# Decay between tokens of a gated delta rule: exp(-|G_t - g_j|) from stored cumulative sums in place of a TensorE product of masked gates

## The chip, the core and the metric

The kernel runs on one core of a Trainium2 chip. The metric is the device time in microseconds of one execution; of three runs before the change the median is 3756.54 us (3755.67 to 3763.35). One execution was profiled; it took 3761.12 us, and its trace spans 3759.3 us.

Engines in the profile: PE is TensorE (PEld its weight loads), DVE VectorE, ACT ScalarE, POOL GpSimd, SP SyncE, which here issues every DMA of the loop. Each runs its own instructions in order and waits on semaphores.

## The reference

The input x has 8 sequences of 1024 tokens, 128 wide. A gated delta-rule attention layer and a feed-forward layer stand one behind the other; each is `x = x + layernorm(layer(layernorm(x)))`. All is float32. The part that matters here, with H = 16 heads, DK = 64, DV = 128:

```python
q, k, v = causal_conv_silu(x @ Wq.T), ..., ...      # 4 taps; q and k are normed over DK
alpha = exp(-exp(A_log) * softplus(x @ Wa.T + dt_bias))
beta = 2.0 * sigmoid(x @ Wb.T)
def step(S, inp):                                   # over the 1024 tokens
    kS = einsum('bhd,bhdv->bhv', k_t, S)
    kkS = einsum('bhd,bhv->bhdv', k_t, kS)
    S = a_t * (S - b_t * kkS) + einsum('bhd,bhv->bhdv', k_t, v_t)
    o_t = einsum('bhdv,bhd->bhv', S, q_t)
o = rms_norm(o) @ Wo.T
```

## The kernel before

The recurrence is computed in chunks of C = 64 tokens. A prologue norms x, transposes it, computes the gates (log alpha in `la`, beta in `be`) and tables of their sums (`tabP`, `tabR`). The main part has STEPS = 128 steps: 8 pairs of heads by 16 chunks, all 8 sequences at once. A tile of 128 partitions holds the 64 tokens of one head in its upper and those of the other in its lower half; along the columns stand the 8 sequences. An epilogue does the feed-forward layer.

A step n runs through three stages, and one pass of the loop does one stage of three neighbouring steps: `l` is finished (inverse applied, output, state S), `m` is in the middle (Gram products, Newton steps for the inverse of a triangular matrix), `n` is begun (projections, convolutions, Gram of k). `pe_body`, `act_body`, `dve_body`, `pool_body` and `sp_body` list what each engine does in a pass, in an order written out by hand; nothing reorders it. 124 passes run in a loop, three bodies stand ahead of it and three behind.

The part that is changed makes the decay between token j and token t of a chunk, the exponential of the sum of log gates between them. Before: POOL multiplies the log gates of step n by two masks (`pool_lm`, tile Lm, 2 x 512 columns); PE multiplies that by triangles of ones, eight products of 256 columns (`pe_dec`, line 513); ACT takes the exponential out of PSUM (`act_exp`, line 726, into ex); POOL multiplies one half by beta over the norm of k (`pool_dmn`, line 995) and the other by the causal mask (`pool_dmp`, line 999). DVE multiplies the Gram product by the first (`dve_n`, line 890, to Nd) and the product of q and k by the second (`dve_p`, line 897, to PT). At the first token of a sequence the gate is set to -1e4 (RESET).

Names on the way: line 502 are the projections (j = 0 to 3: k, q and two halves of v), line 719 the first tap of a convolution on ACT, line 852 the other three on DVE; PE starts projection j + 1 after DVE has done the taps of j, since all use one region of PSUM. Line 696 sums the squares of the output (one-column products), DVE's line 881 reads that, and PE waits for it before line 523, the squared norms of k (one column too). Line 544 is the Gram product of k, line 585 the product N Z, line 611 the product with X0 or X (`pe_z`), line 941 the copy of its diagonal blocks to Z by DVE, line 595 a transpose, line 533 the norms of q, line 706 the output projection, lines 637, 687, 650, 653 are U, the change of S, and the two parts of the output.

Blocks for the inverse go through HBM: `sp_gram` writes Nd (line 1089, scrN), `sp_gram_in` reads 16 x 16 blocks of it (NS), POOL eliminates in them (lines 1047 to 1053), DVE finishes (lines 921 to 931), and SP writes the result (`sp_z_out`, scrZ; `sp_x_out`, line 1108, scrX) and reads it back in another layout: `sp_z_in` (line 1116, Z) and `sp_x_in` (lines 1123 and 1124, X0; the profile calls this tile X). `sp_g` (line 1082) loads two rows of exp(cumulative sum) into every partition of a half of ex, from scrG, which was written once before the loop. A pair of DMAs like this (one for each half) is meant by "pair" below. POOL also scales S (line 1007, Sg) and DVE adds to it (line 960).

Of the kernel before, what the change touches and what calls it, by code (L numbers as in the profile page):

```python
# [15 lines left out]
ALU = mybir.AluOpType  # L16
# [23 lines left out]
RESET = -1.0e4  # L40
# [40 lines left out]
def build(nc, x, wtab, wo, wab, hcol, cst, wf, mu, out):  # L81
    with ExitStack() as ctx:
# [40 lines left out]
        scrX = nc.dram_tensor("scrX", (NB * SB,), F32, kind="Internal").ap()  # L123
        scrG = nc.dram_tensor("scrG", (STEPS, 2, NB * C), F32, kind="Internal").ap()
# [46 lines left out]
        cexp = sig("cexp")  # L171

# [9 lines left out]
        with nc.Block() as block:  # L182
# [32 lines left out]
            def _(dve):  # L215
# [45 lines left out]
                la4 = la[:].rearrange("p (h c b) -> p h c b", h=HP, c=NC)  # L261
                nc.vector.memset(la4[0:1, :, 0, :], RESET)
                then(nc.vector.memset(la4[64:65, :, 0, :], RESET))
# [7 lines left out]
                nc.vector.tensor_copy(tp[:, :, 0:8], v8(la))  # L271
                nc.vector.tensor_scalar(tp[:, :, 8:16], v8(be), -1.0, None, ALU.mult)
                dve.wait_ge(cexp.sem, 1)
                nc.vector.scalar_tensor_tensor(tr[:, :, 0:4], v8(tmp[0])[:, :, 0:4], -1.0, v8(be)[:, :, 0:4], ALU.mult, ALU.mult)
                dve.wait_ge(cexp.sem, 2)
# [77 lines left out]
        g_tr = sig("g_tr")  # L353
        g_cp = sig("g_cp", 2)
        g_out = sig("g_out", 32)
        g_in = sig("g_in", 32)
        lm_ok = sig("lm_ok")
        dec_mm = sig("dec_mm")
# [79 lines left out]
        exN, exP = half(ex, 0), half(ex, 1)  # L438
        CLASSES = (range(0, 4), range(4, 8))
# [643 lines left out]

        def sp_gram(sp, n):
# [67 lines left out]
        def pe_body(pe, l, m, n):  # L1152
# [49 lines left out]
            if m is not None:  # L1202
                if n is not None:
                    pe.wait_ge(dec_ex.sem, dec_ex.at(n))
                else:
                    pe.wait_ge(kt_ok.sem, kt_ok.at(m))
# [32 lines left out]
        def act_body(act, l, m, n):  # L1239
# [112 lines left out]
        with nc.Block() as block:  # L1352
# [277 lines left out]
```

## Time and profile before

| | before |
|---|---|
| median of 3 runs, us | 3756.54 |
| profiled execution, us | 3761.12 |
| its span in the trace, us | 3759.3 |
| mean granted TensorE clock | 0.916 |
| PE busy | 3311.8 us, 88% |
| DVE busy | 2620.1 us, 70% |
| ACT busy | 2675.7 us, 71% |
| POOL busy | 2247.2 us, 60% |
| DMA | 226.12 MB, 60 GB/s |

The busy shares are averages over all stages. An engine at 88% has idle time of a few tenths of a microsecond between groups of instructions; whether such a gap is a wait is told by the row's "[idle before <-releaser]". The granted clock is the share of 2.4 GHz that TensorE was given: 1.00 or 0.50 (1.2 GHz) at a time. Times in the timeline are microseconds from the start of the span; a row merges neighbouring instructions of one kind, with their count.

### The profile page before, as it was taken

How to read it: one execution, taken by the hardware profiler on the slowest of the kernel's cores; microseconds unless marked ns; L12 is line 12 of the kernel's file. 1: busy time of each engine (PE TensorE's matmuls, PEld its weight loads, DVE VectorE, ACT ScalarE, POOL GpSimd, SP SyncE). 2: the span in 40 equal slices, each digit the busy share in tenths (PEclk: the TensorE clock that was granted, in tenths of full speed). 3: DMA queues.
4: the chain of work that ended last, by engine and by line, in shares of the span. 5: the costliest groups of instructions: out<-in, count | busy, mean ns of one | idle time of the engine just before them, and what ended most of it. 6: DMA issues, size and time to landing. Idle time of an engine off the chain costs nothing. (4 is left out here: it accounts for less than half of the span.)

```text
span 3759.3 us, 195058 instructions
## 1 busy us (share of the span) xinstructions
PE 3311.8 (88%) x77978; PEld 2756.6 (73%) x77978; DVE 2620.1 (70%) x5529; ACT 2675.7 (71%) x5548; POOL 2247.2 (60%) x3494
## 2 busy tenths in 40 slices
PE   5699999999999999999999999999999999999665
PEld 4577777777777777777777777777777777777433
DVE  5677777777777777777777777777777777777254
ACT  2577777777777777777777777777777777777433
POOL 1366666666666666666666666666666666666211
PEclk9799999999999999999999999999999999999767
DMA  2232323233232323233232323233232323323111
GB/s 60 51 67 57 69 56 67 59 63 62 61 65 58 69 54 69 61 62 64 59 69 54 70 57 66 59 63 69 54 69 56 67 57 65 62 60 66 34 34 40
DMA packets 911057, 226.12 MB, mean 60 GB/s; under 512 B 820128, under 2 KB 894112, under 8 KB 911008
## 3 DMA queue, kind: packets, MB, share of 16 engines
q1 hardware_dynamic: 910848, 224.91, 28.5%
q8 instruction: 33, 0.54, 0.1%
q0 software_dynamic: 160, 0.53, 0.0%
q14 instruction: 16, 0.13, 0.0%
HBM read 169.73 MB, written 55.58 MB: 60 GB/s over the span
## 5 line engine op out<-in xcount | busy, mean ns | idle before, releaser
L852 DVE SCALAR_TENSOR_TENSOR cv<-ps,w_kq,cv 128x512 f32<-128x512 f32 x768 | 575.6, 750 | 419.2 <-ACT cv L719 405.6
L852 DVE SCALAR_TENSOR_TENSOR cv<-ps,w_v,cv 128x512 f32<-128x512 f32 x768 | 575.7, 750 | 152.8 <-ACT cv L719 134.7
L1016 POOL TENSOR_TENSOR accT<-accT,X 128x512 f32 (+1 forms) x128 | 163.5, 1277 | 533.3 <-ACT Y L817 533.3
L502 PE MATMUL ps<-xnT,w_kq 128*128 (+1 forms) x1024 | 327.6, 445 | 74.6 <-DVE cv L852 68.9
L502 PE MATMUL ps<-xnT,w_v 128*128 (+1 forms) x1024 | 330.8, 448 | 14.2 <-DVE cv L852 14.1
L976 POOL TENSOR_TENSOR sc<-tabP,sc 128x8 f32<-128x8 f32 x128 | 26.1, 204 | 510.5 <-DVE sc L867 510.5
L1007 POOL TENSOR_TENSOR Sg<-S,tabR 128x512 f32<-128x512 f32 x256 | 329.9, 1307 | 0.0
L765 ACT ACTIVATE Vt<-ps,sc 128x128 f32<-128x128 f32 x1024 | 277.8, 382 | 54.9 <-PE ps L571 54.9
L706 PE MATMUL ps<-wo_s,oo 128*128 128x128 f32 x2048 | 312.9, 314 | 0.6 <-issue 0.6
L967 POOL TENSOR_TENSOR Lm<-k_all,tabP 128x512 f32<-128x512 f32 x256 | 280.3, 1114 | 30.5 <-POOLq L182 30.5
L706 PEld LDWEIGHTS ps<-wo_s,oo 128*128 128x128 f32 x2048 | 288.1, 225 | 14.1 <-issue 0.9
L952 DVE SCALAR_TENSOR_TENSOR Rr<-ps,sc,Vt 128x128 f32<-128x128 f32 x1024 | 288.3, 345 | 1.4
L637 PEld LDWEIGHTS ps<-Rr,Z 64*64 64x64 f32 x4096 | 243.7, 144 | 56.2 <-issue 56.2
L696 PEld LDWEIGHTS ps<-k_all,KB 128*128 128x128 f32 x2048 | 239.9, 193 | 58.9 <-issue 58.9
L502 PEld LDWEIGHTS ps<-xnT,w_kq 128*128 128x128 f32 x1024 | 184.1, 199 | 126.6 <-issue 93.2
L637 PE MATMUL ps<-Rr,Z 64*64 64x128 f32 x4096 | 274.8, 288 | 1.9 <-issue 1.9
L696 PE MATMUL ps<-k_all,KB 128*128 128x1 f32 x2048 | 247.4, 251 | 5.9 <-ACT KB L802 2.1
L585 PEld LDWEIGHTS ps<-Z,NM 64*64 64x64 f32 x8192 | 189.2, 168 | 81.1 <-issue 81.0
L585 PE MATMUL ps<-Z,NM 64*64 64x64 f32 x8192 | 215.4, 256 | 31.4 <-DVE Z L941 29.1
L808 ACT ACTIVATE oo<-ps 128x1024 f32<-128x1024 f32 x128 | 131.1, 1024 | 156.6 <-PE ps L653 156.6
L653 PE MATMUL ps<-PT,U 64*64 64x64 f32 x8192 | 217.4, 221 | 23.4 <-PE ps L650 22.8
L817 ACT ACTIVATE X<-ps,sc 128x128 f32<-128x128 f32 x512 | 145.9, 368 | 121.1 <-PE ps L706 120.7
(198 smaller groups left out, 8537.2 us busy)
## 6 DMA issues: line engine op xcount, KB each, us to landing
ex<-scrG SPq DMA_DIRECT2D x256, 128.0 KB, 2.9
scrN<-Nd SPq DMA_DIRECT2D x256, 128.0 KB, 2.6
Z<-scrZ SPq DMA_DIRECT2D x256, 128.0 KB, 3.2
X<-scrX SPq DMA_DIRECT2D x512, 64.0 KB
w_kq<-wtab SPq DMA_DIRECT2D x128, 132.0 KB, 2.2
w_v<-wtab SPq DMA_DIRECT2D x128, 132.0 KB, 2.5
wo_s<-wo SPq DMA_DIRECT2D x128, 128.0 KB, 2.8
NS<-scrN SPq DMA_DIRECT2D x128, 64.0 KB, 2.6
```

Source lines behind the costliest of these rows:

```text
L502: last = nc.tensor.matmul(pj[:, 4 * g:4 * g + 4, 0:CW], w[:, (j % 2) * P:(j % 2 + 1) * P], xnT3[:, 4 * g:4 * g + 4, bass.ds((n % NC) * C, ...
L585: last = nc.tensor.matmul(ps[place(cls, a), col64(PB["y1" if l else "y0"], cls, i)], blk64(BD["NM"], b, a), blk64(BD["Z"], b, a), start=Tr ...
L637: last = nc.tensor.matmul(ps[a:z, col128(PB["u"], g, i)], blk64(BD["Z"], b, a), unit(Rr, b)[a:z], start=True, stop=True)
L653: last = nc.tensor.matmul(o_cols(h ^ cls, b, d), U[a:z, b * P + d:b * P + d + 64], blk64(BD["PT"], b, a), start=False, stop=(b == NB - 1))
L696: last = nc.tensor.matmul(ps[:, (PB["ms"] + h) * 512 + i:(PB["ms"] + h) * 512 + i + 1], osq[:, h * 512 + i * P:h * 512 + (i + 1) * P], kc( ...
L706: last = nc.tensor.matmul(ps[:, col128(PB["wo"], h, i)], oo[:, h * 512 + i * P:h * 512 + (i + 1) * P], wo_s[:, h * D:(h + 1) * D], start=T ...
L765: last = nc.scalar.activation(unit(Vt, b), unit(ps, 4 * PB["vtr"] + b), ACT.Copy, scale=rv[:, b:b + 1])
L852: nc.vector.scalar_tensor_tensor(cv4[:, j], pj[:, :, k:k + C], tap(j, k), cv4[:, j], ALU.mult, ALU.add).then_inc(conv[j].sem, 1)
L952: last = nc.vector.scalar_tensor_tensor(unit(Rr, b), ps[:, col128(PB["ks"], g, i)], cr[:, b:b + 1], unit(Vt, b), ALU.mult, ALU.add)
L967: last = nc.gpsimd.tensor_tensor(v3(Lm, i), over(kc(o, C), NB, C), tabP3[:, bass.ds(n, 1), 0:8].rearrange("p o b -> p b o").to_broadcast([ ...
L1007: nc.gpsimd.tensor_tensor(half(Sg, g).rearrange("p (b v) -> p b v", b=4), half(S, g).rearrange("p (b v) -> p b v", b=4), gam, ALU.mult).th ...
L1016: nc.gpsimd.tensor_tensor(dst, dst, row(yt[h]), ALU.add).then_inc(acc_ok.sem, 1)
```

## The change

The cumulative sums G of the log gates within a chunk are already computed in the prologue, in PSUM (banks 0 to 3). After the change they are kept: for each token in a column of `tabP` (g_j, in place of the log gate), and, transposed, as one row for each step and half in a new HBM tensor scrD. In each step SP loads the two rows of scrD into all 64 partitions of their half of Lm (`sp_d`), POOL subtracts the column (`pool_d`), ACT takes the absolute value and then the exponential with scale -1 (`act_abs`, `act_exp`), in place in SBUF. The gates fall along the tokens, so -|G_t - g_j| is the wanted sum on either side of the diagonal. `pe_dec` and the masks of POOL are gone. The first chunk's reset is done by zeroing table entries in the prologue. Waits of `act_exp` for the readers of ex move to `pool_dmn` and `pool_dmp`.

```diff
@@ the tables, on DVE in the prologue
-                nc.vector.memset(la4[0:1, :, 0, :], RESET)
-                then(nc.vector.memset(la4[64:65, :, 0, :], RESET))
...
-                nc.vector.tensor_copy(tp[:, :, 0:8], v8(la))
...
+                dve.wait_ge(cexp.sem, 2)
+                nc.vector.tensor_copy(tp[:, :, 0:4], bank(0, 2).rearrange("p (n k) -> p n k", k=8)[:, :, 0:4])
+                nc.vector.tensor_copy(tp[:, :, 4:8], p4(6)).then_inc(d_tab.sem, 1)
...
+                then(nc.vector.memset(first_chunk(tmp[0][:], 8), 0.0))
+                dve.sem_inc(g_tab.sem, 1)
+                then(nc.vector.memset(first_chunk(tabR[:], 16)[:, :, 4:16], 0.0))
@@ TensorE
-        def pe_dec(pe, n):
-            pe.wait_ge(lm_ok.sem, lm_ok.at(n))
-            pe.sem_inc(pe_go.sem, 1)
-            for i, o in enumerate((K_LE, K_GT)):
-                for cls in range(2):
-                    for a, z in HALF:
-                        c = (PB["dec"] + cls) * 512 + i * 4 * C
-                        last = nc.tensor.matmul(ps[place(cls, a), c:c + 4 * C], k_all[a:z, o + a:o + z],
-                                                Lm[a:z, i * 512 + cls * 4 * C:i * 512 + (cls + 1) * 4 * C], start=True, stop=True)
-            last.then_inc(dec_mm.sem, 1)
@@ ScalarE
+        def act_abs(act, n):
+            act.wait_ge(d_ok.sem, d_ok.at(n))
+            nc.scalar.activation(Dt, Dt, ACT.Abs).then_inc(d_abs.sem, 1)
+
         def act_exp(act, n):
-            act.wait_ge(dec_mm.sem, dec_mm.at(n))
-            if not first(n):
-                act.wait_ge(nd_ok.sem, nd_ok.at(n - 1))
-                act.wait_ge(pt_ok.sem, pt_ok.at(n - 1))
-            nc.scalar.activation(ex[:, 0:1024].rearrange("p (i g n) -> p g i n", i=2, g=2),
-                                 bank(PB["dec"], 2).rearrange("p (g i n) -> p g i n", g=2, i=2), ACT.Exp).then_inc(dec_ex.sem, 1)
+            act.wait_ge(d_abs.sem, d_abs.at(n))
+            nc.scalar.activation(Dt, Dt, ACT.Exp, scale=-1.0).then_inc(dec_ex.sem, 1)
@@ GpSimd
-        def pool_lm(pool, n):
-            if not first(n):
-                pool.wait_ge(dec_mm.sem, dec_mm.at(n - 1))
+        def pool_d(pool, n):
+            pool.wait_ge(d_in.sem, d_in.at(n))
+            if not first(n):
+                pool.wait_ge(dmn_ok.sem, dmn_ok.at(n - 1))
+                pool.wait_ge(dmp_ok.sem, dmp_ok.at(n - 1))
             pool.sem_inc(pool_go.sem, 1)
-            for i, o in enumerate((K_MGT, K_MLE)):
-                last = nc.gpsimd.tensor_tensor(v3(Lm, i), over(kc(o, C), NB, C),
...
+            nc.gpsimd.tensor_tensor(v3(Lm, 1), v3(Lm, 0),
+                                    tabP3[:, bass.ds(n, 1), 0:8].rearrange("p o b -> p b o").to_broadcast([P, NB, C]),
+                                    ALU.subtract).then_inc(d_ok.sem, 1)
@@ SyncE
+        def sp_d(sp, n):
+            if not first(n):
+                sp.wait_ge(d_ok.sem, d_ok.at(n - 1))
+            sp.sem_inc(sp_go.sem, 1)
+            for h, (a, z) in enumerate(HALF):
+                sp.dma_start(half(Lm, 0)[a:z], scrD[bass.ds(n, 1), h, :].to_broadcast([C, NB * C])).then_inc(d_in.sem, 16)
@@ before the loop: SP, ACT and PE (eight more transposes, two copies, two writes)
+            for h, n in enumerate(("Z", "X0")):
+                sp.wait_ge(d_cp.sem, d_cp.at(0, h + 1))
+                sp.dma_start(scrD[:, h, :], half(BD[n], 1)).then_inc(d_out.sem, 16)
...
+            sp.wait_ge(d_out.sem, d_out.at(0))
@@ the bodies
         def sp_body(sp, l, m, n):
+            if n is not None:
+                sp_d(sp, n)
             if l is not None:
                 sp_x_in(sp, l)
...
-                pe_dec(pe, n)
```

Three places in the order of the instructions show it. First PE in the loop, around the product that goes; S and sl are the state and the convolved k, KB the squared output, sq squares. Before:

```order
L626 MATMUL ps<-S,sl 64x128 [waits s1_ok,silu_k,s0_ok]
L626 MATMUL ps<-S,sl 64x128 x15
L507 REGISTER_ALU [waits kt_ok]
L513 MATMUL ps<-Lm,k_all 64x256 [waits lm_ok]
L513 MATMUL ps<-Lm,k_all 64x256 x7
L696 MATMUL ps<-k_all,KB 128x1 [waits pt_ok,osq_ok]
L696 MATMUL ps<-k_all,KB 128x1 x7
L523 MATMUL ps<-k_all,sq 64x1 [waits ro_in,sq_k]
L523 MATMUL ps<-k_all,sq 64x1 x15
L502 MATMUL ps<-xnT,w_v 128x4x67 [waits conv_q,wv_in]
```

and now, from the same product with S on:

```order
L623 MATMUL ps<-S,sl 64x128 [waits s1_ok,silu_k,s0_ok]
L623 MATMUL ps<-S,sl 64x128 x15
L693 MATMUL ps<-k_all,KB 128x1 [waits pt_ok,osq_ok]
L693 MATMUL ps<-k_all,KB 128x1 x7
L515 REGISTER_ALU [waits ro_in]
L520 MATMUL ps<-k_all,sq 64x1 [waits sq_k]
L520 MATMUL ps<-k_all,sq 64x1 x15
```

Line 513 is gone with its wait for POOL, and line 696 (now 693) follows the product with S at once; line 523 (now 520) still waits for ro_in, which DVE signals.

Second SP at the head of a pass, where X stands for X0, w_kq for the weights of k and q, and Nd for the Gram product. Before:

```order
L1346 UNCONDITIONAL_BRANCH
L1346 ISA
L1121 ISA [waits x_out]
L1123 DMA X<-scrX 64x4x64 [waits z_mm]
L1124 DMA X<-scrX 64x4x64
L1123 DMA X<-scrX 64x4x64
L1124 DMA X<-scrX 64x4x64
L1061 ISA
L1063 ISA [waits conv_q]
L1063 DMA w_kq<-wtab 128x264
L1089 DMA scrN<-Nd 64x8x64 [waits n_in,nd_ok]
```

and now:

```order
L1353 UNCONDITIONAL_BRANCH
L1353 ISA
L1091 ISA [waits d_ok]
L1091 DMA Lm<-scrD 64x512
L1091 ISA
L1091 DMA Lm<-scrD 64x512
L1128 ISA
L1130 ISA [waits x_out]
L1132 DMA X<-scrX 64x4x64 [waits z_mm]
L1133 DMA X<-scrX 64x4x64
L1132 DMA X<-scrX 64x4x64
L1133 DMA X<-scrX 64x4x64
```

The pair from scrD stands ahead of the four DMAs of X0 and of all that comes behind them.

Third ACT, where sl is the convolved k, sq its square, and sc holds the small columns of norms. Before:

```order
L719 ACTIVATE cv<-ps,w_kq 128x512 [waits silu_q,proj_q]
L730 ISA
L736 ACTIVATE sl<-cv 128x512 [waits k_tr,gram_p,ks_mm,gram_k,conv_k]
L742 ACTIVATE sq<-sl 128x512 [waits nk_mm,silu_k]
L1260 ACT_TABLE_LOAD
L726 ACTIVATE ex<-ps 128x2x2x256 [waits pt_ok,nd_ok,dec_mm]
L825 ACTIVATE sc<-sc 128x8 [waits v_ok,n2_ok]
```

and now:

```order
L733 ACTIVATE sl<-cv 128x512 [waits k_tr,gram_p,ks_mm,gram_k,conv_k]
L739 ACTIVATE sq<-sl 128x512 [waits nk_mm,silu_k]
L720 ACTIVATE Lm<-Lm 128x512 [waits d_ok]
L1267 ACT_TABLE_LOAD
L724 ACTIVATE Lm<-Lm 128x512 [waits d_abs]
L822 ACTIVATE sc<-sc 128x8 [waits v_ok,n2_ok]
L826 ACTIVATE sc<-sc 128x8 [waits rv_ln]
```

The exponential out of PSUM has become an Abs ahead of the table load and an exponential behind it, each of 512 columns.

## Rows read from the trace of the kernel before

**Rows 1.** Timeline of PE: last group of line 653 in five steps (start, us).

```profile
613.89 0.69 PE L653 MATMUL ps<-PT,U 64*64 64x64 f32 x32 [0.18 <-PE ps L650]
...
639.08 0.69 PE L653 MATMUL ps<-PT,U 64*64 64x64 f32 x32 [0.18 <-PE ps L650]
...
665.45 0.69 PE L653 MATMUL ps<-PT,U 64*64 64x64 f32 x32 [0.18 <-PE ps L650]
...
693.43 0.69 PE L653 MATMUL ps<-PT,U 64*64 64x64 f32 x32 [0.18 <-PE ps L650]
...
719.73 0.69 PE L653 MATMUL ps<-PT,U 64*64 64x64 f32 x32 [0.18 <-PE ps L650]
```

**Rows 2.** Windows: stretch, length, busy by engine, then granted clock, DMA share, GB/s.

```profile
614.60:639.80 25.20, 22.80 (x601) 19.28 (x601) 18.93 (x38) 20.06 (x42) 16.20 (x27) 1.00 0.33 65
...
614.60:720.50 105.90, 97.24 (x2401) 81.91 (x2402) 76.56 (x149) 80.09 (x169) 68.63 (x109) 0.94 0.31 62
647.70:651.10 3.40, 3.40 (x69) 2.49 (x68) 2.19 (x8) 2.63 (x6) 2.66 (x4) 0.50 0.50 111
...
685.30:688.70 3.40, 3.40 (x20) 2.50 (x21) 0.73 (x1) 1.97 (x4) 2.93 (x9) 0.50 0.00 0
```

**Rows 3.** Groups of instructions by line, shapes apart: busy us, mean ns.

```profile
L513 PE MATMUL ps<-Lm,k_all 64*64 64x256 f32 x2048 | 139.1, 381 | 2.4 <-DVE KT L903 1.6 <-POOL Lm L967 0.5
...
L726 ACT ACTIVATE ex<-ps 128x1024 f32<-128x1024 f32 x128 | 131.0, 1023 | 1.4
...
L742 ACT ACTIVATE sq<-sl 128x512 f32<-128x512 f32 x128 | 80.7, 630 | 4.0
```

**Rows 4.** Timeline of DVE: last two taps of q, then line 881.

```profile
644.15 1.53 DVE L852 SCALAR_TENSOR_TENSOR cv<-ps,w_kq,cv 128x512 f32<-128x512 f32 x2
...
646.40 0.17 DVE L881 TENSOR_TENSOR sc<-ps,sc 128x8 f32<-128x8 f32 x1 [0.71 <-PE ps L696]
```

**Rows 5.** Timeline of SP's queue, 618 to 626 us.

```profile
618.01 1.28 SPq L1116 DMA_DIRECT2D Z<-scrZ  x2
619.55 1.21 SPq L1082 DMA_DIRECT2D ex<-scrG  x2
...
623.32 0.62 SPq L1124 DMA_DIRECT2D X<-scrX  x1
624.38 0.34 SPq L1063 DMA_DIRECT2D w_kq<-wtab  x1
625.26 1.28 SPq L1089 DMA_DIRECT2D scrN<-Nd  x2
```

**Rows 6.** DMA issues: count, KB each, median us from issue to landing.

```profile
ex<-scrG SPq DMA_DIRECT2D x256, 128.0 KB, 2.9
...
Z<-scrZ SPq DMA_DIRECT2D x256, 128.0 KB, 3.2
...
w_kq<-wtab SPq DMA_DIRECT2D x128, 132.0 KB, 2.2
...
scrX<-XB SPq DMA_DIRECT2D x128, 64.0 KB, 2.6
```

**Rows 7.** Timeline of PE: the product with X0, step of 25.19 us.

```profile
626.60 0.69 PE L611 MATMUL ps<-Y,X 64*64 64x64 f32 x32 [0.27 <-ACT Y L780]
```

**Rows 8.** The same product in the step of 27.98 us.

```profile
679.34 0.69 PE L611 MATMUL ps<-Y,X 64*64 64x64 f32 x32
```

**Rows 9.** Timeline of DVE: the update of S and what follows it.

```profile
640.04 1.29 DVE L960 TENSOR_TENSOR S<-ps,Sg 128x512 f32<-128x512 f32 x2 [0.18 <-POOL Sg L1007]
...
641.70 0.69 DVE L903 TENSOR_TENSOR KT<-ps,tabP 128x512 f32<-128x512 f32 x1 [0.37 <-PE ps L564]
...
642.89 0.75 DVE L852 SCALAR_TENSOR_TENSOR cv<-ps,w_kq,cv 128x512 f32<-128x512 f32 x1 [0.50 <-ACT cv L719]
```

**Rows 10.** Timeline of SP's queue before the loop.

```profile
93.31 0.36 SPq L1129 DMA_DIRECT2D scrG<-Y  x1
95.63 0.34 SPq L1063 DMA_DIRECT2D w_kq<-wtab  x1
```

More of the change, by code:

```diff
@@ L123, in build @@
         scrX = nc.dram_tensor("scrX", (NB * SB,), F32, kind="Internal").ap()
+        scrD = nc.dram_tensor("scrD", (STEPS, 2, NB * C), F32, kind="Internal").ap()
         scrG = nc.dram_tensor("scrG", (STEPS, 2, NB * C), F32, kind="Internal").ap()
@@ L171, in build @@
         cexp = sig("cexp")
+        d_tab = sig("d_tab")
+        g_tab = sig("g_tab")
         xt = [KBuf for KBuf in (BD["KB"], BD["QG"])]
@@ L352, in build @@
         wo_in = sig("wo_in", 16)
-        g_tr = sig("g_tr")
+        g_tr = sig("g_tr", 2)
         g_cp = sig("g_cp", 2)
+        d_cp = sig("d_cp", 2)
         g_out = sig("g_out", 32)
         g_in = sig("g_in", 32)
-        lm_ok = sig("lm_ok")
-        dec_mm = sig("dec_mm")
+        d_out = sig("d_out", 32)
+        d_in = sig("d_in", 32)
+        d_ok = sig("d_ok")
+        d_abs = sig("d_abs")
         dec_ex = sig("dec_ex")
@@ L438, in build @@
         exN, exP = half(ex, 0), half(ex, 1)
+        Dt = half(Lm, 1)
         CLASSES = (range(0, 4), range(4, 8))
@@ L994, in pool_dmn @@
             pool.wait_ge(bn_ok.sem, bn_ok.at(n))
-            nc.gpsimd.tensor_tensor(v3(ex, 0), v3(ex, 0), bcast(bn, C), ALU.mult).then_inc(dmn_ok.sem, 1)
+            if not first(n):
+                pool.wait_ge(nd_ok.sem, nd_ok.at(n - 1))
+            nc.gpsimd.tensor_tensor(v3(ex, 0), v3(Lm, 1), bcast(bn, C), ALU.mult).then_inc(dmn_ok.sem, 1)
         def pool_dmp(pool, n):
             pool.wait_ge(dec_ex.sem, dec_ex.at(n))
-            nc.gpsimd.tensor_tensor(v3(ex, 1), v3(ex, 1), over(kc(K_MLE, C), NB, C), ALU.mult).then_inc(dmp_ok.sem, 1)
+            if not first(n):
+                pool.wait_ge(pt_ok.sem, pt_ok.at(n - 1))
+            nc.gpsimd.tensor_tensor(v3(ex, 1), v3(Lm, 1), over(kc(K_MLE, C), NB, C), ALU.mult).then_inc(dmp_ok.sem, 1)
         def pool_sg(pool, m):
@@ L1082, in sp_g @@
                 sp.dma_start(half(ex, 2)[a:z], scrG[bass.ds(n, 1), h, :].to_broadcast([C, NB * C])).then_inc(g_in.sem, 16)
+        def sp_d(sp, n):
+            if not first(n):
+                sp.wait_ge(d_ok.sem, d_ok.at(n - 1))
+            sp.sem_inc(sp_go.sem, 1)
+            for h, (a, z) in enumerate(HALF):
+                sp.dma_start(half(Lm, 0)[a:z], scrD[bass.ds(n, 1), h, :].to_broadcast([C, NB * C])).then_inc(d_in.sem, 16)
         def sp_gram(sp, n):
@@ L1202, in pe_body @@
             if m is not None:
[L1203 to L1206, printed above, removed]
+                pe.wait_ge(kt_ok.sem, kt_ok.at(m))
                 pe_y(pe, m, 0)
@@ L1321, in pool_body @@
             if n is not None:
-                pool_lm(pool, n)
+                pool_d(pool, n)
             if m is not None:
@@ L1365, in _ @@
                 act.preload_act_table_set("silu_and_others")
+                act.wait_ge(g_tr.sem, g_tr.at(0, 1))
+                for h, n in enumerate(("Z", "X0")):
+                    nc.scalar.activation(v3(BD[n], 1), bank(2, 2).rearrange("p (b h t) -> p b h t", b=NB, h=2)[:, :, h, :],
+                                         ACT.Copy).then_inc(d_cp.sem, 1)
                 act.wait_ge(g_tr.sem, g_tr.at(0))
@@ L1378, in _ @@
                 for b in range(NB):
+                    last = nc.tensor.transpose(unit(ps, 8 + b), tabP3[:, :, b], ident)
+                last.then_inc(g_tr.sem, 1)
+                for b in range(NB):
                     last = nc.tensor.transpose(unit(ps, 16 + b), tmp[0][:].rearrange("p (n b) -> p n b", b=NB)[:, :, b], ident)
                 last.then_inc(g_tr.sem, 1)
+                pe.wait_ge(d_cp.sem, d_cp.at(0))
                 pe.wait_ge(g_cp.sem, g_cp.at(0))
```

14 lines of the change are left out of this document (3 added, 11 removed).

## The prediction

> **What bounds the kernel now.** I read the engine table first, then the timeline of four neighbouring steps, then its windows for the clock, and last the two engines that meet there, TensorE (PE) and the queue of SyncE (SP). A "step" is one pass of the loop; I count it from the start of the last 32 products of line 653, which end every step. Five such starts lie 25.19, 26.37, 27.98 and 26.30 us apart [rows 1]: a beat of 105.84 us, 26.46 us a step. The windows say why the four differ [rows 2]: over the beat the granted clock is 0.94, and inside it stand stretches at 0.50 (1.2 GHz instead of 2.4). The shortest step has none. A first kind of stretch (647.7 to 651.1, and one like it in each of the next two steps) comes right behind the one-column products of lines 696 and 523; a second kind (685.3) stands in the 27.98 step alone, behind line 533, also one-column products. A stretch of the first kind costs 26.30 - 25.19 = 1.11 us, the second kind 27.98 - 26.30 = 1.68 us. PE is busy in nearly all of the rest, so this is a PE-bound loop whose queue is fed in a fixed order: what counts is which wait on PE ends last, place by place. There are 124 passes of the loop, and three bodies before and three behind them.
>
> **What goes: the product of masked gates.** Per step PE loses the eight products of line 513: 139.1 us over 128 steps, 1.09 us each [rows 3]. If PE alone bound, that is -136 us. It does not follow, since behind it PE waits for VectorE (DVE). Line 696 would start 1.1 us earlier and end 1.1 us earlier, but line 523 waits for DVE's line 881, and DVE does the three taps of the q convolution first: they end at 644.15 + 1.53 = 645.68, while line 881 starts now at 646.40, after an idle 0.71 us [rows 4]. So at most 0.7 of the 1.09 us passes this place; the rest is a new wait of PE for DVE.
>
> **What ScalarE (ACT) gets.** One exponential of 1024 columns from PSUM (1023 ns) becomes an Abs and an Exp of 512 each in SBUF; the nearest row is line 742, 630 ns [rows 3]. 2 x 0.63 - 1.02 = +0.24 us. The Abs stands ahead of the table load, so the Exp ends some 0.25 us later than now. Both ends: 0 (there is idle time before line 825) and 0.25 us. I take 0.25: it leaves 0.7 - 0.25, about 0.4 us, of the gain for what comes after. GpSimd (POOL) replaces two products by one subtraction, at a place where it isn't waited for; it gains about 1 us that nobody needs.
>
> **What SP gets.** Two DMAs of scrD into Lm per step, of the same form as the pair from scrG into ex (64 rows of 2 KB each out of one row): 1.21 us of issue, and 0.26 us between the end of the pair before (618.01 + 1.28) and its start [rows 5]. 1.47 us a step. Their data are wanted some 20 us later, so the transfer is hidden. The queue behind them is not: they stand at the head of the body, ahead of the four DMAs that bring X0 from scrX, then w_kq, then the pair that writes Nd out. SP runs without a pause from the issue of scrX to the last of the four (they follow one another at 618.01, 619.55, ... 623.32), so the four move by the full 1.47 us: the last one starts at 624.79 instead of 623.32. How long it takes to land the page doesn't say of this one; its twin in size, scrX<-XB of 64 KB, takes 2.6 us, and the ends are w_kq, 2.2, and Z, 3.2 [rows 6]. With 2.6: X0 is there at 625.9 now and at 627.39 after.
>
> Line 611 (the product of X0 with Y) starts at 626.60 in the step without a slow stretch [rows 7]. Now X0 has 0.7 us to spare; after, PE stands there until 627.4, 0.8 us later than now, whatever it gained before. With the landing at 2.2 it is 0.4 us, at 3.2 it is 1.4 us. Does the delay stay on the path? DVE's copy of Z follows the product, and line 585 needs the copy, then come line 595, 533 and 611 again, the v projection's taps, and the next step. Each waits for the one before; there is no slack after line 611 in this step. So 25.19 + 0.8 = 26.0 us.
>
> In the steps with a slow stretch of the first kind line 611 comes later anyway: at 679.34, 13.9 us after its step's start at 665.45, against 12.7 in the free step [rows 1, 7, 8]. X0 after the change: 627.4 - 613.89 = 13.5. There the 0.4 us gained before does count: 26.3 becomes 25.9, and as the slow stretch can now begin earlier and lie over more of the v projection (line 502), I give 0.1 back: 26.0. So X0 makes all steps equal at 26.0 us, but for the second kind of slow stretch.
>
> The third thing on SP: the pair that writes Nd starts at 625.26 now, right when Nd is ready; after, SP comes to it at 624.38 + 0.34 + 1.47 + 0.1, about 626.3, +1.0 us. It feeds POOL's elimination, after which POOL scales S, and DVE's update of S at 640.04 already waits 0.18 us for that [rows 9]. It moves to 641.1 where the step's end moves to 640.6: 0.5 us late. DVE has waits of 0.37 and 0.50 us before the next two operations, so I price it at 0, with 0.3 us as the other end.
>
> **The clock.** Taking 1.09 us of dense products out from right before the one-column products leaves the thin stretch longer: lines 696 and 523 with a wait between. The row shows the clock at 0.50 after this place in three steps of four [rows 2]; it will be all or nearly all, which costs nothing more, since X0 hides it (above). What decides is the second kind, in one step of four now. PE's new wait before line 611 stands ahead of it, and as the steps become equal their phase is a new one. Bounds: never (0) and every step (1.68 us). I take 0.35 instead of 0.25 of the steps.
>
> The Trainium skill (TensorE: Matmul & The Clock Gate, What's actually happening) says that the slow clock is the default and activity releases it. By that rule removing dense products and adding a wait can only bring more slow stretches; rows 2 agree as far as they go, every fall stands behind one-column products.
>
> **The sum.** A step after: 26.0 + 0.35 x 1.68 = 26.6 us, against 26.46: +0.14, times 124 = +17 us. The prologue: eight more transposes ahead of the eight of G, two ACT copies and two more writes to HBM before the wait for both (scrG is issued at 93.31, w_kq at 95.63 after it has landed [rows 10]): about 2 us; the first pair from scrD ahead of w_kq, for which PE waits: 1.5 us; two copies out of PSUM and two memsets in DVE's chain: 2 us, an estimate from 0.6 to 0.7 us for 512 columns [rows 3, 4]; together +5.5. Own time of the profiled execution 3761.1 + 17 + 5.5 = 3784. The median of the runs is 3756.5, 4.6 below that execution. **Forecast: 3780 us.**
>
> **Rivals.**
> 1. *The queue of SP isn't the bound; the kernel is faster.* X0 lands in 2.2 us or less and SP catches up somewhere, so that PE keeps what passes DVE, 0.3 to 0.4 us a step: 0.35 x 124 = 43, minus 5.5: 3756.5 - 38 = 3718 us. For it: 1.09 us of PE work really goes from the bounding engine. Against: SP's rows have no gap in which 1.47 us fit between scrX and X0 [rows 5]. The Trainium skill (DMA: Bandwidth & Descriptors, Issuing engines are not separate DMA queues) calls the sequencer's time to start a DMA usually small beside the DMA; here a pair holds SP 1.21 us, and one of the pair lands in 2.9 [rows 5, 6]. By that rule this rival is the forecast.
> 2. *The clock.* The second kind of slow stretch comes in three steps of four: 26.0 + 0.75 x 1.68 = 27.3, +0.8 x 124 = +100, and with the prologue 3860 us. It decides from one step in two on (26.84, +0.38 x 124 = +47, 3809). For it: the thin part of the step grows; against: it falls in a part of the step that the edit itself leaves as it is.
> 3. *No change.* The loss in the free step and the gain in the others cancel, with the second kind still in one of four: 26.0 + 0.42 = 26.42, -5 us in the loop, +5.5 in the prologue: 3757 us.
>
> **Chances.** Forecast (3765 to 3810) 0.48, rival 1 0.22, rival 2 0.17, rival 3 0.13. What a measurement can tell from no change is about 0.2%, 7.5 us. Faster 0.22, same 0.13, slower 0.65. The range takes rival 1 down to 3715 and rival 2 up to 3850: landing times of 2.2 and 3.2 us alone move the free step by -0.4 and +0.6 us, and one step in ten more or less of the second kind is 21 us.
>
> **What would show it.** Line 611's first product waiting for the DMA X<-scrX in most steps, and starting 13.5 us after the step's start in nearly all of them; the four X0 issues 1.47 us later against scrX's; Nd's write starting about 1 us after Nd is ready; DVE's update of S waiting for POOL; line 523 still waiting for DVE's line 881; the count of slow stretches of the second kind a beat. Wrong if PE doesn't wait for X0 (then rival 1), or if the steps are equal at 26.0 and yet the time is far from 3780 (then the clock).

## The result, and the profile after

| | before | after |
|---|---|---|
| median, us | 3756.78 (3755.67 to 3763.35, 4 runs) | 3881.47 (3875.72 to 3882.07, 4 runs) |
| ratio to before | | 1.0325 [1.0307, 1.0343] |
| span of the profiled execution, us | 3759.3 | 3879.8 |
| mean granted TensorE clock | 0.916 | 0.881 |
| PE busy | 3311.8 us | 3311.0 us |

The kernel became 3.3% slower. I had forecast 3780 us with a range from 3715 to 3850: the sign was right, the size was not. After the change the lines have moved: 653 is now 650, 696 is 693, 523 is 520, 533 is 530, 611 is 608, DVE's 881 and 897 are 878 and 894, SP's 1124, 1063 and 1089 are 1133, 1065 and 1098.

Timeline of PE in the kernel after, four steps (start us, length us, engine, line, operation, out<-in, tile, type, count [idle before <-releaser]):

```profile
1615.56 0.69 PE L650 MATMUL ps<-PT,U 64*64 64x64 f32 x32 [0.18 <-PE ps L647]
...
1643.26 0.69 PE L650 MATMUL ps<-PT,U 64*64 64x64 f32 x32 [0.18 <-PE ps L647]
...
1671.33 0.69 PE L650 MATMUL ps<-PT,U 64*64 64x64 f32 x32 [0.18 <-PE ps L647]
...
1676.64 1.92 PE L693 MATMUL ps<-k_all,KB 128*128 128x1 f32 x16 [0.90 <-DVE PT L894]
1679.01 0.64 PE L520 MATMUL ps<-k_all,sq 64*64 64x1 f32 x32 [0.45 <-DVE sc L878]
...
1697.80 0.69 PE L650 MATMUL ps<-PT,U 64*64 64x64 f32 x32 [0.18 <-PE ps L647]
...
1725.89 0.69 PE L650 MATMUL ps<-PT,U 64*64 64x64 f32 x32 [0.18 <-PE ps L647]
```

The steps are 27.70, 28.07, 26.47 and 28.09 us long. Before they were 25.19, 26.37, 27.98 and 26.30 [rows 1]. The short one is gone, and two of the four are about 28.

Windows of the kernel after (stretch, length, busy of PE, PEld, DVE, ACT, POOL, then granted clock, DMA share, GB/s): the four steps, then the slow stretches in the first, third and fourth of them.

```profile
1616.30:1726.60 110.30, 97.95 (x2337) 83.17 (x2337) 78.69 (x149) 80.62 (x172) 65.78 (x106) 0.89 0.32 69
1622.10:1628.80 6.70, 6.25 (x108) 5.15 (x107) 3.50 (x14) 4.24 (x8) 2.98 (x5) 0.50 0.54 151
1680.20:1683.40 3.20, 3.20 (x68) 2.39 (x67) 2.00 (x7) 2.50 (x7) 2.77 (x4) 0.50 0.51 132
1707.50:1710.70 3.20, 3.20 (x65) 3.08 (x59) 2.48 (x6) 2.94 (x4) 2.57 (x4) 0.50 0.47 107
1717.70:1721.00 3.30, 3.30 (x18) 2.39 (x20) 0.49 (x1) 2.02 (x4) 2.64 (x10) 0.50 0.00 0
```

Beside the two kinds of slow stretch known from before [rows 2] there is a long form of the first: from 1622.1 to 1628.8, twice as long, beginning while line 693 still runs. The lengths of 120 inner steps, each from one start of the last group of line 650 (653 before) to the next:

| steps | before | after |
|---|---|---|
| no slow stretch | 32 of 25.19 us | 1 of 25.75 |
| first kind alone | 61 of 26.33 | 49 of 26.43 |
| first kind, long | none | 32 of 27.70 |
| first and second kind | 27 of 27.99 | 37 of 28.09 |
| long and second | none | 1 of 29.63 |
| mean, us | 26.40 | 27.30 |

From the first such start to the last, 3361.9 us before and 3478.3 after: +116.4 us lie in the steps, some 108 of them in these 120 and some 8 in the first and the last few. Of the rest of the +120.5 by which the span grew, 4.0 us lie ahead of them, and nothing behind.

By this table the +0.90 us a step is made up of four parts. Before, 32 steps were 1.14 us shorter than those with the first kind alone, and all but one of these are gone: 0.30. After, 33 steps have the long form, 1.27 us each: 0.35. Eleven more have the second kind, 1.66 us each: 0.15. And with the same slow stretch a step is 0.10 us longer than before.

Waits of the kernel after (who waited for whom: us in total, times, longest):

```profile
PE ps L693 <- DVE PT L894: 112.7, 125, 0.9
...
PE ps L520 <- DVE sc L878: 56.8, 126, 0.5
```

and its line 608, by line (busy us, mean ns | idle before, by releaser):

```profile
L608 PE MATMUL ps<-Y,X 64*64 64x64 f32 x8192 | 179.2, 225 | 4.6 <-DMA X<-scrX 4.4 <-ACT Y L777 0.2
```

These rows together are the balance. The removed products were 139.1 us of PE [rows 3], and yet PE's busy time is the same (3311.8 and 3311.0 us): the remaining work took that much longer at the lower mean clock (0.881 for 0.916). Where the products stood, line 693 now waits for DVE's P^T, for 112.7 us in all, a wait that the kernel before does not have. PE's idle time, span less busy, grew from 447.5 to 568.8 us, by 121.3 us, which is the whole loss. PE waits for X0 for 4.4 us in the whole run; it isn't X0 that made the kernel slow.

A small part of the loss has nothing to do with the clock. Before, line 523 starts 0.15 us after DVE's line 881 has ended; now line 520 starts 0.25 us after the end of line 878, in every one of the 120 steps, and PE's wait for it grew from 44.1 to 56.8 us:

```profile
PE ps L523 <- DVE sc L881: 44.1, 126, 0.4
```

That is the 0.10 us between 26.33 and 26.43. In the order of the instructions the wait for ro_in has moved from the product itself to an instruction of its own ahead of it (L515 REGISTER_ALU); that this is what takes the 0.1 us was not tested.

### The profile page after: what moved, and what is told of

Read it like the earlier page. It is cut to its first block and busy times, and to the rows that moved or that the text cites. A ratio compares the mean times of both kernels' runs of the same rounds, so it can differ in the third digit from the quotient of the medians.

```text
span 3879.8 us, 191739 instructions
## 1 busy us (share of the span) xinstructions
PE 3311.0 (85%) x75938; PEld 2780.3 (72%) x75938; DVE 2663.5 (69%) x5530; ACT 2692.0 (69%) x5678; POOL 2124.0 (55%) x3366
## 5 line engine op out<-in xcount | busy, mean ns | idle before, releaser
L510 PE MATMUL ps<-xnT,w_kq 128*128 (+1 forms) x1024 | 337.5, 456 | 76.8 <-DVE cv L849 68.9
L693 PE MATMUL ps<-k_all,KB 128*128 128x1 f32 x2048 | 264.7, 259 | 114.9 <-DVE PT L894 112.7
L510 PE MATMUL ps<-xnT,w_v 128*128 (+1 forms) x1024 | 356.1, 476 | 4.2 <-DVE cv L849 4.1
L693 PEld LDWEIGHTS ps<-k_all,KB 128*128 128x128 f32 x2048 | 257.5, 204 | 142.2 <-issue 142.2
L703 PE MATMUL ps<-wo_s,oo 128*128 128x128 f32 x2048 | 328.0, 324 | 1.4 <-DVE Rr L949 1.4
L703 PEld LDWEIGHTS ps<-wo_s,oo 128*128 128x128 f32 x2048 | 303.5, 235 | 16.3 <-issue 1.6
L1009 POOL TENSOR_TENSOR Sg<-S,tabR 128x512 f32<-128x512 f32 x256 | 308.6, 1226 | 0.0
L582 PEld LDWEIGHTS ps<-Z,NM 64*64 64x64 f32 x8192 | 202.2, 178 | 88.9 <-issue 88.9
L582 PE MATMUL ps<-Z,NM 64*64 64x64 f32 x8192 | 227.6, 267 | 38.3 <-DVE Z L938 38.3
L1018 POOL TENSOR_TENSOR accT<-accT,Y 128x512 f32 (+1 forms) x128 | 242.0, 1891 | 0.2 <-issue 0.2
```

What stands on the lines that cost most here:

```text
L510: last = nc.tensor.matmul(pj[:, 4 * g:4 * g + 4, 0:CW], w[:, (j % 2) * P:(j % 2 + 1) * P], xnT3[:, 4 * g:4 * g + 4, bass.ds((n % NC) * C, ...
L582: last = nc.tensor.matmul(ps[place(cls, a), col64(PB["y1" if l else "y0"], cls, i)], blk64(BD["NM"], b, a), blk64(BD["Z"], b, a), start=Tr ...
L693: last = nc.tensor.matmul(ps[:, (PB["ms"] + h) * 512 + i:(PB["ms"] + h) * 512 + i + 1], osq[:, h * 512 + i * P:h * 512 + (i + 1) * P], kc( ...
L703: last = nc.tensor.matmul(ps[:, col128(PB["wo"], h, i)], oo[:, h * 512 + i * P:h * 512 + (i + 1) * P], wo_s[:, h * D:(h + 1) * D], start=T ...
L1009: nc.gpsimd.tensor_tensor(half(Sg, g).rearrange("p (b v) -> p b v", b=4), half(S, g).rearrange("p (b v) -> p b v", b=4), gam, ALU.mult).th ...
L1018: nc.gpsimd.tensor_tensor(dst, dst, row(yt[h]), ALU.add).then_inc(acc_ok.sem, 1)
```

## The experiments

The theory after the result: the loss is TensorE's clock, which falls behind the products of one column (lines 693, 520 and 530), and removing the dense products in front of them only laid bare more of it. Its rival is my forecast's own mechanism, the longer queue of SP. "Widened" means that a product of one column gets 64 or 128 equal columns. Each experiment's ratio is to the kernel before, run on the same chip in the same job.

| kernel | median, us | ratio [95%] | mean step, us | none | first | long | second |
|---|---|---|---|---|---|---|---|
| before | 3756.78 | 1 | 26.40 | 32 | 88 | 0 | 27 |
| after | 3881.47 | 1.0325 [1.0307, 1.0343] | 27.30 | 1 | 86 | 33 | 38 |
| e1_fill | 3832.48 | 1.0196 [1.0143, 1.0249] | 26.98 | 16 | 88 | 4 | 44 |
| e2_spmove | 3875.88 | 1.0307 [1.0284, 1.0329] | 27.30 | 0 | 91 | 29 | 41 |
| e4_before_wide | 3625.46 | 0.9649 [0.9626, 0.9671] | 25.35 | 120 | 0 | 0 | 0 |
| e7_ms4 | 3875.71 | 1.0315 [1.0290, 1.0340] | 27.30 | 0 | 68 | 52 | 67 |
| e5_after_wide | 3700.14 | 0.9853 [0.9837, 0.9870] | 25.93 | 120 | 0 | 0 | 0 |
| e6_wide_sp | 3642.34 | 0.9701 [0.9682, 0.9721] | 25.43 | 120 | 0 | 0 | 0 |
| e8_all | 3535.47 | 0.9418 [0.9402, 0.9435] | 24.57 | 120 | 0 | 0 | 0 |
| e9_wide_first | 3815.36 | 1.0176 [1.0151, 1.0201] | 26.79 | 48 | 0 | 0 | 72 |
| e10_wide_nq | 3877.41 | 1.0323 [1.0288, 1.0357] | 27.31 | 0 | 40 | 80 | 0 |
| e11_wide_ms4 | 3717.56 | 0.9889 [0.9856, 0.9922] | 26.05 | 101 | 0 | 0 | 0 |

The last four columns count, in 120 inner steps of the profiled execution, those without a slow stretch, those with the first kind in its short and in its long form (beginning up to 10.5 us after a step's end of line 650, or its like), and those with the second kind (from 16.5 us on). e11 has 19 steps with a stretch between the two, at 14 us.

**e1_fill: the dense products back, and nothing else.** After, with eight products of 256 columns on constants at the old place, into PSUM banks that nobody reads then.

```diff
+    if m is not None:
+        pe.wait_ge(kt_ok.sem, kt_ok.at(m))
+    pe_fill(pe, n)     # 8 products 64x256, k_all x k_all, banks 4 and 5
     if l is not None:
```

> The changed kernel with eight products of 256 columns put back where the old ones stood, on constants, their result used by nobody; all else (loads, subtraction, Abs and Exp) as changed. Theory clock: the products gave no time as work, but they kept TensorE's clock up ahead of the one-column products; steps without a slow stretch come back, PE then waits for X0 in them: 25.9, 26.4, 28.0, 26.4 us, about 3795 us. Rival SP queue (the loss is the late X0 and Nd): nothing changes or it gets 0.1 us a step worse, 3880 to 3895 us.

Measured 3832 us. Adding work that nobody needs makes the kernel 1.3% faster, which no queue explains, and the mean clock rises from 0.881 to 0.905; so far the theory holds. But the size is short of the 3795. Steps without a slow stretch came back in 16 of 120, not in 32, and they last 25.85 us, not 25.19: X0 is late in them. e1's line 617 (608 of after) waits for it:

```profile
PE ps L617 <- DMA X<-scrX: 34.6, 31, 3.7
```

So dense products ahead of the thin ones help the clock here, and don't secure it. The same products at another place weren't tried, so this run alone doesn't tell whether it is their place that counts.

**e2_spmove: the two loads of scrD behind everything that this step needs.**

```diff
 def sp_body(sp, l, m, n):
-    if n is not None:
-        sp_d(sp, n)
     ...
         sp_gram_in(sp, m)
+    if n is not None:
+        sp_d(sp, n)
```

> The changed kernel with the pair of loads from scrD issued later in SP's body, behind the read of the 16x16 blocks (where SP waits anyway), so that X0, w_kq and Nd are issued as before the change. Theory clock: X0 is hidden behind the slow stretch in nearly every step, so 3870 to 3882 us. Rival SP queue: the whole loss goes, about 3765 us.

The last issue of X0 ends 1.4 us earlier in the step than after the change, the mean step stays at 27.30, the time is 3876 us. The queue, as the kernel stands, costs nothing of note. The rival's 3765 is out.

**e4_before_wide: the kernel before, thin products made wide.** The moving operand has 64 or 128 equal columns, of which one is read.

```diff
-  nc.tensor.matmul(ps[:, (PB["ms"] + h) * 512 + i:(PB["ms"] + h) * 512 + i + 1],
-                   osq[:, ...], kc(K_ONE, 1), start=True, stop=True)
+  nc.tensor.matmul(ps[:, col128(PB["ms"], h, i)],
+                   osq[:, ...], kc(K_ONE), start=True, stop=True)
```

and likewise lines 523 and 533 with 64 columns.

> The kernel before the change, with the sums of squares (lines 523, 533, 696) taken by moving tiles of 64, 64 and 128 equal columns instead of one; the first column of each result is read. The same number of instructions, the same values. Theory clock: nearly all slow stretches go, all steps as the free one, 25.2 us: 3757 - 1.25 x 124 = about 3600 us. Rival (slow stretches come with the time of the step or with waits, not with one-column products): the wider tiles cost 0.1 to 0.3 us a step, 3770 to 3795 us.

Measured 3625 us, 3.5% faster than before; 25 us more than expected, since the step is 25.35 us, not 25.2. Timeline of its PE, and a window over four steps:

```profile
1603.49 0.69 PE L653 MATMUL ps<-PT,U 64*64 64x64 f32 x32 [0.18 <-PE ps L650]
...
1608.80 2.02 PE L696 MATMUL ps<-k_all,KB 128*128 128x128 f32 x16
1611.17 0.69 PE L523 MATMUL ps<-k_all,sq 64*64 64x64 f32 x32 [0.35 <-DVE sc L881]
...
1628.81 0.69 PE L653 MATMUL ps<-PT,U 64*64 64x64 f32 x32 [0.18 <-PE ps L650]
```
```profile
1603.00:1704.00 101.00, 92.09 (x2396) 76.94 (x2388) 75.41 (x149) 80.27 (x169) 68.61 (x109) 1.00 0.32 65
```

Sixteen products of 128 columns take 2.02 us, of one column 1.92 at the full clock; 32 of 64 columns 0.69 instead of 0.64. For a tenth of a microsecond here and there the clock stays at 2.4 GHz through all 120 steps. The waits in this place are the same as in the free step before (0.35 us for line 881), so it is the columns, not the waits. The Trainium skill (TensorE: Matmul & The Clock Gate, HAM oscillation — how this bites in real kernels) describes a clock that swings because the engine stands idle for DMA. That is another case than this one: after the change, PE stands idle for 0.45 us in all, and not for a DMA, between the start of line 693 at 1676.64 and the fall at 1680.2; and e5_after_wide, below, keeps both idle gaps of this place (113.2 and 56.7 us in all, 112.7 and 56.8 after), and has no slow stretch in 120 steps.

**e7_ms4: the wait for P^T taken away.** The sums of line 693 go to PSUM banks 4 and 5, which are free once DVE has copied K^T; in banks 2 and 3 they had to wait for P^T to be read.

```diff
-PB = {..., "ms": 2, "wo": 6}
+PB = {..., "ms": 4, "wo": 6}
-            pe.wait_ge(pt_ok.sem, pt_ok.at(m))
+            pe.wait_ge(kt_ok.sem, kt_ok.at(m))
         pe_ms(pe, l)
```

> The changed kernel with the sums of the squared output (line 693) written to PSUM banks 4 and 5, which the removed products freed, so that they need not wait for DVE's PT but only for KT. Theory clock: PE's wait of 0.9 us ahead of them goes, but the thin stretch gets no denser; line 520 waits for DVE's line 878 instead, some 0.6 us earlier than now: between 3800 (the 0.6 us counts) and 3881 us (the slow stretches take it back); I expect 3830. Rival (the wait for PT is the whole loss): below 3790 us.

A miss: the time lies inside the two bounds, but at the end where nothing is gained, not at 3830. The wait is gone, and line 693 starts 4.34 us after the group's start instead of 5.31, but the time is what it was. Timeline of its PE, then the two slow stretches in the second step:

```profile
2051.16 0.69 PE L650 MATMUL ps<-PT,U 64*64 64x64 f32 x32 [0.18 <-PE ps L647]
2055.50 1.95 PE L693 MATMUL ps<-k_all,KB 128*128 128x1 f32 x16
...
2076.86 0.69 PE L650 MATMUL ps<-PT,U 64*64 64x64 f32 x32 [0.18 <-PE ps L647]
...
2105.73 0.69 PE L650 MATMUL ps<-PT,U 64*64 64x64 f32 x32 [0.18 <-PE ps L647]
```
```profile
2083.80:2090.50 6.70, 6.70 (x108) 5.66 (x109) 4.56 (x14) 5.06 (x10) 2.98 (x5) 0.50 0.56 142
2097.50:2100.80 3.30, 3.30 (x18) 2.39 (x20) 0.49 (x1) 2.07 (x4) 2.79 (x8) 0.50 0.00 0
```

The steps are mostly 25.8, 27.3 and 28.8 us long: those with the short first kind alone are 0.64 us shorter than after the change (25.79 for 26.43), and the clock, at 0.861, takes all of it back, with the second kind in 67 steps for 38. Removing work or waits from PE does not pay here while the clock falls.

**e5_after_wide, e6_wide_sp, e8_all: the change at full clock, one cover after the other.** e5 widens lines 693, 520 and 530 of the changed kernel as e4 does; e6 adds e2's move; e8 adds e7's banks as well.

> The changed kernel, but lines 520, 530 and 693 multiply by 64, 64 and 128 equal columns in place of one (only one of them is read). Theory (the lost time is TensorE's clock, which falls where the products have one column): no stretch with a clock of 1.2 GHz stays in the loop. Then the transfer of the value projection (X0, which lands 12.5 us after the end of a step's value chain) sets every step, at about 25.8 us as in the few full-clock steps of e1_fill, 1.5 us under the 27.3 of the changed kernel: about 3695 us (3680 to 3710). Rival A, the late transfer binds nothing even at full clock: 25.35 us a step as in e4_before_wide, about 3635 us. Rival B, the clock's fall comes from the removed products alone and not from the one-column ones: 3840 to 3880 us.

> As e5_after_wide, and the two decay loads of the next chunk moved on SP's queue behind the transfers that this step needs. If the late X0 is what e5_after_wide's steps wait for, these go to 25.35 us as in e4_before_wide and the whole to its 3625 us and some 8 to 12 us of longer prologue: 3635 to 3640 us. If X0 doesn't bind there, this is the same as e5_after_wide within 5 us.

> As e6_wide_sp, and the sums of the squared output go to PSUM banks that the matrices of the tail don't use, so that TensorE doesn't wait for DVE's copy of P^T (as in e7_ms4). Theory (the removed 1.09 us of products lay in the shadow of that wait, and comes out once both the wait and the clock's falls are gone): a step of 24.7 to 24.9 us, 3560 to 3590 us. Rival (something behind the q convolution, GpSimd's S or the transfers, sets the step at once): 25.35 us as e6_wide_sp, 3635 us.

e5 came to 3700 (expected 3695), e6 to 3642 (3635 to 3640). Line 608 in both, by line, e5 first:

```profile
L608 PE MATMUL ps<-Y,X 64*64 64x64 f32 x8192 | 178.6, 224 | 101.3 <-DMA X<-scrX 100.2 <-issue 0.8 <-ACT Y L777 0.3
```
```profile
L608 PE MATMUL ps<-Y,X 64*64 64x64 f32 x8192 | 178.6, 224 | 37.6 <-ACT Y L777 33.0 <-DMA X<-scrX 3.4 <-issue 1.1
```

With the clock out of the way X0 does bind, for 100.2 us, 0.8 a step; with the pair moved on SP, PE waits for X0 for 3.4 us, and the kernel is 58 us faster. A step of e5, timeline of PE:

```profile
1773.94 0.69 PE L650 MATMUL ps<-PT,U 64*64 64x64 f32 x32 [0.18 <-PE ps L647]
1779.25 2.02 PE L693 MATMUL ps<-k_all,KB 128*128 128x128 f32 x16 [0.90 <-DVE PT L894]
...
1787.28 0.69 PE L608 MATMUL ps<-Y,X 64*64 64x64 f32 x32 [0.64 <-DMA X<-scrX]
...
1799.73 0.69 PE L650 MATMUL ps<-PT,U 64*64 64x64 f32 x32 [0.18 <-PE ps L647]
```

e5 against e4 is the change as it was made, with both kernels at full clock: 3700 against 3625 us, +75 us (2.1% by the ratios) instead of the +125 with the clock falling, and 58 of the 75 go with the pair's place on SP. With the clock falling the same move was worth some 6 us at most (e2; the intervals overlap). So the clock and the late X0 can't be booked side by side.

e6 against e4 is the change alone, at full clock and with its queue put right: 0.9701 [0.9682, 0.9721] against 0.9649 [0.9626, 0.9671], each to the kernel before in its own job; it is slower by 0.5%, mostly the 0.08 us a step. That is about the 0.09 us by which line 520 starts later in e6 than line 523 in e4 (medians of 7.78 and 7.69 us into the step). The removed 1.09 us a step are worth nothing there: the wait for P^T stands in their place (e6: 113 us), and line 693 starts 5.31 us into the step in e6, as line 696 does in e4 (5.32). e8 takes that wait away and comes to 3535 us, under its expected 3560 to 3590, and 5.8% under the kernel before. Its PE:

```profile
1670.10 0.69 PE L650 MATMUL ps<-PT,U 64*64 64x64 f32 x32 [0.18 <-PE ps L647]
...
1674.43 2.05 PE L693 MATMUL ps<-k_all,KB 128*128 128x128 f32 x16
1677.01 0.69 PE L520 MATMUL ps<-k_all,sq 64*64 64x64 f32 x32 [0.53 <-DVE sc L878]
...
1694.64 0.69 PE L650 MATMUL ps<-PT,U 64*64 64x64 f32 x32 [0.18 <-PE ps L647]
```

24.54 us a step: of the 0.98 us by which line 693 starts earlier 0.85 us arrives at the mean step. This is where the gain of the removed products had been: it takes the wide columns, the moved pair and the other banks together. Before, the same banks held their result until the exponential had read it, so e8's step isn't open to the kernel before as it stands; a version of that kernel with other banks wasn't tried.

**e9_wide_first and e10_wide_nq: which thin products.** e9 widens lines 693 and 520 only, e10 line 530 only.

> As e5_after_wide, but only lines 520 and 693 are widened; the norms of q at line 530 keep one column. Theory (each run of one-column products brings its own fall of the clock): the slow stretch at 6 to 9 us into a step is gone, the one at 18 to 20 us stays, in about one step in three; steps of 25.8 and of about 27.5 us: some 3770 us (3740 to 3800). Rival (line 530 doesn't matter, the first run of one-column products alone starts both): as e5_after_wide, about 3695 us.

> The changed kernel with only line 530 (the norms of q) widened to 64 equal columns; lines 520 and 693 keep one. The counterpart of e9_wide_first. If each run of one-column products brings its own fall of the clock, the slow stretch at 18 to 20 us into a step goes and the one at 6 to 9 us stays in every step: about 26.4 us a step, 3775 us (3755 to 3795). If it is the sum of the thin products over a step that counts, wherever they stand, stretches stay at both places, and the time lies between 3790 and 3860 us.

Windows of e9 over a slow stretch and the whole step around the next but one; then of e10 over two slow stretches and the two steps around them:

```profile
746.90:750.20 3.30, 3.30 (x26) 2.61 (x27) 1.63 (x3) 2.12 (x4) 2.64 (x10) 0.50 0.00 0
...
782.60:809.90 27.30, 23.63 (x585) 19.83 (x585) 19.70 (x37) 20.44 (x43) 16.08 (x26) 0.94 0.34 70
```
```profile
1563.50:1570.20 6.70, 6.25 (x106) 5.14 (x107) 3.90 (x13) 4.43 (x9) 2.98 (x5) 0.50 0.54 144
1594.20:1597.50 3.30, 3.30 (x62) 3.18 (x54) 2.58 (x5) 2.88 (x4) 2.51 (x4) 0.50 0.51 117
1557.40:1611.50 54.10, 48.01 (x1168) 40.97 (x1168) 38.24 (x75) 40.22 (x86) 31.93 (x53) 0.91 0.33 71
```

"Run" here means a row of one-column products behind one another. As to places both say the same: each such row brings its own stretch. In e9 the first kind is gone from all steps, in e10 the second. As to the time both missed. e9 has the second kind in 72 of 120 steps, not in one of three (3815 us for 3770). e10 lost the second kind altogether and gained nothing (3877 for 3775): 80 of its 120 steps have the long form of the first kind, against 33 after. The two don't add up. Taking one away moves the steps against the clock, and the other comes more often or lasts longer; only without both is the time gone. What sets how often they come, and why some are twice as long, these runs don't show.

**e11_wide_ms4: the wait gone, X0 still late.** e5 with e7's banks.

> As e5_after_wide, and the sums of the squared output in banks 4 and 5 as in e8_all, but the decay loads of the next chunk stay ahead of X0 on SP's queue. If X0's landing 12.5 us into the step sets e5_after_wide's steps, then taking away TensorE's wait for P^T buys nothing: 25.8 us a step, 3700 us as e5_after_wide. If that wait is worth the 0.85 us a step by which e8_all is under e6_wide_sp, whatever X0 does: about 3595 us.

3718 us: nothing gained over e5. It is 0.4% slower, measured in another job; a slow stretch is back in 19 steps. By line:

```profile
L608 PE MATMUL ps<-Y,X 64*64 64x64 f32 x8192 | 180.5, 226 | 208.4 <-DMA X<-scrX 207.1 <-issue 0.8 <-ACT Y L777 0.5
```

207.1 us of waiting for X0 are about e5's 100.2 and the 113 us that it had at P^T, moved to one place.

## Why the prediction was wrong

**What failed first: "What goes".** I let 0.7 of the removed 1.09 us pass, up to DVE's line 881. But line 696 itself waits for P^T; that wait stood with it in the order of the program, and I priced only what came behind it. In the free step before, line 696 starts 619.21 - 613.89 = 5.32 us after the group; after, 1676.64 - 1671.33 = 5.31. Timeline of the kernel before, PE and DVE, then of DVE after:

```profile
618.09 1.07 PE L513 MATMUL ps<-Lm,k_all 64*64 64x256 f32 x16
...
618.38 0.68 DVE L897 TENSOR_TENSOR PT<-ps,ex 128x512 f32<-128x512 f32 x1
...
619.21 1.92 PE L696 MATMUL ps<-k_all,KB 128*128 128x1 f32 x16
```

```profile
1675.81 0.68 DVE L894 TENSOR_TENSOR PT<-ps,ex 128x512 f32<-128x512 f32 x1
```

DVE ends P^T at 619.06 before and at 1676.49 after, 5.17 and 5.16 us into the step, and in both kernels the one-column products start 0.15 us later; over the 120 steps the medians are the same, 5.16 and 5.31. Nothing of the 1.09 us passed. The removed products, which end at 619.16, had lain beside DVE's work on P^T to the last, and the row of before showed no wait only because they filled it. So "0.4 us left", and with it "26.3 becomes 25.9" in the slow steps, falls: they are 26.43.

**What failed second: "The clock".** I wrote that the first kind in nearly all steps "costs nothing more, since X0 hides it". It is in all but one, and it costs: X0 would have held a step at 26.0 by the forecast (25.9 in e5), and the slow stretch makes it 26.43. And I had no long form of it, 27.70 - 26.43 = 1.27 us more, in 33 of 120 steps. The frequency of the second kind, 0.35 a step, was about right: 38 of 120, 0.32, at 28.09 - 26.43 = 1.66 us, for my 1.68. That was luck: no row gave the 0.35, and the equal steps by which I argued for it did not come. With the measured terms the step is 26.43 + 0.32 x 1.66 + 0.275 x 1.27 = 27.31, against 27.30 measured and 26.6 forecast; the missing 0.7 us is 0.43 from the first kind (which holds the failed step above) and 0.35 from its long form, less 0.06 from the second. Rival 2 named the clock and 27.3 us a step, but by the second kind in three steps of four; that is not what happened.

**The sign.** "Slower" came true, but not for the reason given. The forecast's +17 us in the loop rested on X0 holding every step at 26.0 us, and on the 0.35 for which no row spoke; PE waits for X0 only twice, for 4.4 us in all. That the sign was right is largely luck.

**What was right but hidden: SP and X0.** The pair takes 1.14 us of issue (timeline of SP, L1091), the last X0 issue moves by 1.25 us for my 1.47, and line 608 starts 1787.28 - 1773.94 = 13.34 us into e5's step for my 13.5. The step that this gives, 26.0, is 25.93 in e5's mean. The mechanism is shown, its price is 58 us (e5 against e6), and in the changed kernel it is covered by the slow clock. The Trainium skill (DMA: Bandwidth & Descriptors, Issuing engines are not separate DMA queues) calls the sequencer's time to start a DMA usually small beside the DMA itself. Here the pair takes 1.14 us to issue and one of it lands 2.8 us after its issue (median of Lm<-scrD), and its place on SP is worth 1.6% once nothing covers it.

**The rest.** ACT's Abs delays the exponential by 0.1 us, not 0.25. The write of Nd is late by 0.8 us (1.0 forecast), and it does cost nothing: DVE's line 957 waits for POOL 1.3 us in the whole run (line 960 before: 6.0). The prologue: w_kq is issued at 99.71 instead of 95.63 [rows 10], +4.1 for my 5.5:

```profile
98.40 1.21 SPq L1091 DMA_DIRECT2D Lm<-scrD  x2
99.71 0.52 SPq L1065 DMA_DIRECT2D w_kq<-wtab  x1
```

Of the two signs that I named for being wrong, "the steps are equal at 26.0 and yet the time is far" and "PE doesn't wait for X0", the second came true, but with a slower kernel instead of a faster one behind it: I had not thought that something slower than X0 could cover it.

## What to carry to other kernels

A row of an engine without a wait may be filled exactly by the work that you remove: look at the semaphores of the instruction behind it, and at when their releaser ends, before a microsecond is booked as gain. On a PE-bound loop read the granted clock first: where it falls behind one-column products, try to widen these (three lines, -3.5% here) before any work is taken from PE; in this loop what was taken out until then came back as a slower clock (the change itself, and e7). A late transfer, a wait and a slow clock cover one another; their prices show only with the others removed, and gains come in jumps when the last cover goes (under e5: e11 nothing, e8 165 us).

## What the runs showed of the hardware

- The width of the moving tile decided over the clock in this loop, at nearly no cost in time. Mean of one product of line 696, 128x1 in the kernel before and 128x128 in e4: 251 ns at a mean clock of 0.916, 282 ns at 0.972; for its 16, 1.92 against 2.02 us at full clock. The columns don't set the pace of these products. The weight loads beside them take 193 ns each in both kernels, and in the step at 613.89 they are busy for 1.86 of the 1.92 us; that they set it was not tested.
- Work whose result nobody reads made a kernel faster (e1, 3832 against 3881 us), with the mean clock at 0.905 for 0.881.
- In two kernels the clock's falls repeat with the loop: before, they mostly come again every four steps [rows 1, 2], in e10 every three, without an exception in 120 (two steps of 27.72 and one of 26.48). After the change no such beat holds: steps of 28.09 and 26.43 us alternate for a while, then some of 27.70 come in between; in e1, e7 and e9 the order is irregular too.
- Time taken from the loop need not show: e7's line 693 starts 1 us earlier in the step than after the change, and the mean step is the same 27.30.
